# A last stage of attention and recurrence: VectorE takes the gated output earlier in even tiles, and one sum out of PSUM ahead of two statistics

## What is computed

```python
x = x + ln(window_attention(ln(x)))
x = x + ln(mixture_of_experts(ln(x)))        # 2 of 8 experts, and a shared expert
x = x + ln(linear_attention(ln(x)))          # gated, causal
x = x + ln(recurrence(ln(x)))                # two steps of a gated cell, then h
```

```python
y  = w0 * expert0 + w1 * expert1 + shared            # the experts' sums, per token
q, k = rotate(silu(x @ Wq)), rotate(silu(x @ Wk));  v = x @ Wv
out  = causal(q @ k.T) @ v                           # with a running state over chunks
out  = (out @ Wo) * sigmoid(x @ G1 @ G2)             # gated output, then a layer norm
c = f * c + i * tanh(...)                            # gates f, i, twice
h = tanh(x @ wo.T + c @ uo.T + bo)                   # for both halves of the sequence
```

## Time and profile before

| | before |
|---|---|
| median of 3 runs | 1473.22 us (1470.95 to 1474.95) |
| the profiled execution's own time | 1473.82 us |
| its span in the profile | 1472.0 us |
| granted TensorE clock, mean | 0.986 |
| TensorE busy | 1414.0 us (96%) |
| VectorE busy | 870.7 us (59%) |
| ScalarE busy | 714.7 us (49%) |
| GpSimd busy | 603.4 us (41%) |

### The profile page before, as it was taken

The page is one execution under the profiler, slowest core; times in us unless marked ns, Lnnn a source line. Parts: engine busy times, 40 slices in busy tenths (PEclk is TensorE's granted clock), DMA queues, the critical chain, the costliest instruction groups (busy, mean ns, idle before and its releaser), DMA issues. The chain is left out here.

```text
span 1472.0 us, 36241 instructions
## 1 busy us (share of the span) xinstructions
PE 1414.0 (96%) x13257; PEld 1237.0 (84%) x13257; DVE 870.7 (59%) x1979; ACT 714.7 (49%) x1656; POOL 603.4 (41%) x1133
## 2 busy tenths in 40 slices
PE   7999999899999999999999998998999999999995
PEld 6888888788999999999999997876777778777874
DVE  5888887364334433343333331366888888888763
ACT  4666665222444444544445442344555555555543
POOL 3665565124112212111221111545667776775342
PEclk9999999899999999999999999999999999999998
DMA  6434333343111111111111111621121212121000
GB/s 193 121 109 128 113 106 120 92 144 113 37 44 38 43 44 51 41 41 44 44 40 48 44 44 61 184 69 47 42 62 45 62 54 61 45 62 38 9 9 29
DMA packets 88732, 100.10 MB, mean 68 GB/s; under 512 B 12432, under 2 KB 75664, under 8 KB 88560
## 3 DMA queue, kind: packets, MB, share of 16 engines
q1 hardware_dynamic: 80704, 78.51, 17.0%
q0 software_dynamic: 6480, 17.70, 4.2%
q10 hardware_dynamic: 1376, 1.57, 0.3%
HBM read 63.28 MB, written 34.47 MB: 66 GB/s over the span
## 5 line engine op out<-in xcount | busy, mean ns | idle before, releaser
L1049 DVE TENSOR_TENSOR ex_gT<-ex_gT,wa_xk 128x256 f32<-128x256 f32 x71 | 29.9, 421 | 305.7 <-ACT ex_gT L1012 305.7
L913 POOL COPY slot_idx<-source 128x1 int32<-128x1 int32 x69 | 37.4, 542 | 402.8 <-PE wa_Z L971 402.8
L944 PE MATMUL wa_P<-ex_xT,lane_w 128*128 128x128 f32 x1704 | 201.9, 275 | 0.0
L980 PE MATMUL wa_Y<-w,ex_gT 128*128 x852 | 195.7, 379 | 1.6 <-DVE ex_gT L1051 1.6
L944 PEld LDWEIGHTS wa_P<-ex_xT,lane_w 128*128 128x128 f32 x1704 | 196.1, 192 | 0.2 <-issue 0.2
L980 PEld LDWEIGHTS wa_Y<-w,ex_gT 128*128 128x128 f32 x852 | 156.3, 190 | 20.1 <-issue 1.8
L944 PE MATMUL wa_qv<-ex_xT,lane_w 128*128 128x128 f32 x852 | 118.2, 275 | 0.0
L944 PEld LDWEIGHTS wa_qv<-ex_xT,lane_w 128*128 128x128 f32 x852 | 111.9, 192 | 3.6
L940 ACT COPY lane_w<-w 128x1408 f32 x71 | 96.9, 1365 | 7.8 <-issue 1.6
L1010 ACT ACTIVATE ex_gT<-wa_qv 128x256 f32<-128x256 f32 x71 | 27.2, 383 | 130.2 <-PE wa_qv L944 130.1
L1117 POOL TENSOR_SCALAR la_ln_ve<-la_ln_mv 128x1 f32<-128x1 f32 x128 | 33.0, 258 | 139.1 <-DVE la_ln_mv L1110 135.0
(11 more groups left out here) (284 smaller groups left out, 3322.8 us busy)
## 6 DMA issues: line engine op xcount, KB each, us to landing
yg<-ex_yo SPq DMA_DIRECT2D x71, 128.0 KB, 1.7
w<-in_w SPq DMA_DIRECT2D x16, 384.0 KB, 4.9
w<-in_w SPq DMA_DIRECT2D x16, 352.0 KB, 3.1
w<-in_w SPq DMA_DIRECT2D x16, 320.0 KB, 4.0
wa_xa<-in_x SPq DMA_DIRECT2D x32, 128.0 KB, 2.1
x<-wa_xo SPq DMA_DIRECT2D x32, 128.0 KB, 1.7
xn<-wa_xn SPq DMA_DIRECT2D x32, 128.0 KB, 3.7
xn1T<-wa_x1T SPq DMA_DIRECT2D x32, 128.0 KB, 2.1
```

The costliest lines, as they stand in the source:

```text
L913: e.tensor_copy(d["idx"][:], source[:, i:i + 1]).then_inc(S["idx"], 1)
L944: o = e.matmul(out, lane_w[:, i % 2, k, at:at + P], B[i % 2]["xT"][:, k, :], start=(k == 0), stop=(k == KC - 1))
L980: o = e.matmul(yb[:, 0:C], gT[:, k, :], w2[:, bass.ds(KF * y + k, 1), :], start=(k == 0), stop=(k == KF - 1))
```

## The change

Two things move in VectorE's code, and no instruction is added or taken away.

- The gated output `y` (now in a helper, `gated_output`) is issued between the two experts' sums in even tiles. In odd tiles it is issued after the second sum, ahead of that sum's statistics. Before, it stood behind those statistics, and in steps 5 to 8 behind the product `fg` too.
- `ucb` is issued ahead of the statistics with the tags x and 3. Before, it stood behind them. `h` stays behind them.

```diff
+        def gated_output(e, i):
+
+            d = B[i % 2]
+            e.wait_ge(S["z"], i + 1)
+            e.wait_ge(S["gt"], i + 1)
+            e.tensor_tensor(d["y"][:], bE[:, 3, 0:C], d["gt"][:], ALU.mult).then_inc(S["y"], 1)
+
...
+                for i in tile(s, 5, NT):
+                    if i % 2 == 0:
+                        gated_output(e, i)
+                for i in tile(s, 1, NT):
+                    d, t = B[i % 2], i // 2 + i % 2 * PAIRS
                     e.wait_ge(S[f"a1{i % 4}"], 16 * (i // 4 + 1))
                     e.wait_ge(S["y0"], i + 1)
                     e.scalar_tensor_tensor(d["ym"][:], YG[1][i % 4][:], weight[:, 1, t:t + 1], d["ym"][:], ALU.mult,
                                            ALU.add).then_inc(S["y1"], 1)
+                for i in tile(s, 5, NT):
+                    if i % 2:
+                        gated_output(e, i)
+                for i in tile(s, 1, NT):
                     e.wait_ge(S["y1"], i + 1)
-                    norm_stats(e, S, "0", i, d["ln0"], d["ym"][:], 3)
+                    norm_stats(e, S, "0", i, B[i % 2]["ln0"], B[i % 2]["ym"][:], 3)
...
                 for i in tile(s, 5, NT):
-                    d = B[i % 2]
-                    e.wait_ge(S["z"], i + 1)
-                    e.wait_ge(S["gt"], i + 1)
-                    e.tensor_tensor(d["y"][:], bE[:, 3, 0:C], d["gt"][:], ALU.mult).then_inc(S["y"], 1)
                     e.wait_ge(S["y"], i + 1)
-                    norm_stats(e, S, "1", i, d["ln1"], d["y"][:], 2)
+                    norm_stats(e, S, "1", i, B[i % 2]["ln1"], B[i % 2]["y"][:], 2)
...
+                for u in pair(s, 11):
+                    e.wait_ge(S["uo"], u + 1)
+                    e.tensor_tensor(H[u % 2]["ucb"][:], carry_bank(u), bo[:], ALU.add).then_inc(S["ucb"], 1)
                 for i in tile(s, 2, NT):
...
                 for u in pair(s, 11):
                     p = H[u % 2]
-                    e.wait_ge(S["uo"], u + 1)
-                    e.tensor_tensor(p["ucb"][:], carry_bank(u), bo[:], ALU.add).then_inc(S["ucb"], 1)
                     e.wait_ge(S["ucb"], u + 1)
```

## The result

| | before | change |
|---|---|---|
| median, same chip, 16 runs each | 1474.64 us | 1477.38 us |
| lowest to highest | 1470.54 to 1477.99 | 1472.40 to 1482.56 |
| span of the profiled execution | 1472.0 us | 1474.8 us |
| mean granted TensorE clock in it | 0.986 | 0.988 |

The ratio is 1.0026, with a 95% interval of 1.0017 to 1.0035: slower by 2.7 us over the medians. That is less than the 0.3% which the prediction took for what can be told from no change, and yet the interval leaves 1 out. The change's profiled execution took 1476.71 us.

The account below looks back on a forecast made before the run. TensorE, nearly always busy, bounds the kernel, waiting in steady state only for `y`, with VectorE having little room before `em`. Collision 2.7, steps 13 and 31 -0.8, early steps 3.5: +5.4 on 1473.2, so 1478.6 us; range 1472.0 to 1482.5.

Parts of the forecast that it names:

- `y` early, even tiles, "nothing gained": Steady even-tile steps: TensorE's 0.63 us cost of waiting for `y` becomes an equally long wait for `em0`.
- The collision: Steady even-tile steps: GpSimd's final sum holds VectorE's second experts' sum by 0.34 us, +2.7 us over eight steps.
- Steps 13 and 31: Their waits hold 1.1 us more than two common ones; early `y` passes that excess, -0.8 us for both together.
- Early steps: Steps 6, 7, 9 and 11, where TensorE does not wait for `y`: work put ahead of `em` costs +3.5 us.
- Odd-tile steps: Steady odd-tile steps: VectorE some 0.4 us late but within 0.49 of room, so nothing; bound 0.1 in each of ten.
- `ucb`: Early `ucb` is worth nothing by itself; at its old place it would be due just as the candidate gate wants it.
- Rival 1: Even-tile steps: second sum not held, runs in 0.48 us; +2.7 us in all, 1475.9 us; chance 0.28.
- rival 3: TensorE's wait for `y` goes and none takes its place: -7.4 us, 1465.8 us; chance 0.12.
- rival 2: Even-tile second sum held longer: rule's full 0.53, +6.9 us; both halves of GpSimd's sum first, +10.7; chance 0.14.

Follow-up runs that it names:

- the first four experiments: Change plus GpSimd's final sum first, 0.9998; before plus even-tile `y` only, 1.0062; before plus odd-tile `y` and `ucb`, 1.0008; change with old `y` in steps 5 to 12, 1.0017.
- all three edits: The change with GpSimd's final sum ahead of its gathers, `y` early only from step 13, `h` late; 1488.67 us against 1488.13, ratio 0.9992; later chip 0.9982.

## Why the prediction was right, point by point

The forecast was 1478.6 us, 5.4 above the 1473.2 then known; measured was 1477.38, 2.7 above its own comparison. The trace has +5.6 for the steps that the sum speaks of. The mechanism held part by part. That the total came so near has luck in it: two misses in the even-tile steps cancel, and 2.8 us given back in the drain, of which the sum knew nothing, meet a comparison that came out 1.4 us higher than the 1473.2.

- ***`y` early, even tiles, "nothing gained"***: the wait for `y` became one for `em0`. Of the same length to 0.14 us: with no hold the step takes 14.79, not 14.93. Start of `y` after L1381: 1.07 foreseen, 1.06 measured. L1319 after the start of `em`: 0.82 and 0.83.
- ***The collision***: right in place, engine and order, too small in size: 0.49 a step and not 0.34. The order is a matter of 0.09 us, by which GpSimd comes first. What was mis-sized is GpSimd's lead: the sum had 0.18 us (1203.62 to 1203.80). The end came as the `la_c` row has it. The first half of L1785 takes 0.74 us from 1207.84 on, and the second sum ends at 1208.90, 0.32 us behind the end of that half (`la_c`: 0.29). By the letter of the Trainium skill's rule (SBUF — State Buffer, Who interferes with whom), that the first to lock the port keeps it for its whole instruction, the full 0.48 us would have come behind that end. So the trace agrees with the rule in that the one that comes first is not held (the run with `h` moved), and not in the full length after. That 0.49 lies nearer to the 0.53 reckoned by the rule is chance. That one with a single SBUF input does not contend, agrees too: before, `y`, one of whose inputs is in PSUM, starts 0.45 us behind GpSimd's final sum and takes 0.42 us. With the gain of 0.14 above, both misses cancel: +0.35 a step against +0.34, 2.8 for eight steps against 2.7.
- ***Steps 13 and 31***: -0.9 against -0.8. The sum of step 13 is held as well (0.98 us), a ninth time that the prediction did not count; in 31 it is not (0.48), since the final sum, with no gathers ahead of it, is long over.
- ***Early steps***: 0.36, 1.48, 0.81 and 0.45 against 0.6, 1.5, 0.8 and 0.6: 3.1 against 3.5. The count by instructions behind `y` less room held; in steps 6 and 11 the room was a little larger than taken.
- ***Odd-tile steps***: 0.05 each, some 0.6 in all, against nothing, within the bound of 0.1 each.
- ***`ucb`***: nothing by itself, and due as the candidate gate wants it, as one experiment shows (6.5 us of waits without the move).
- **The rivals.** Rival 1 (not held) is out by the 0.97 us of the sum, rival 3 (the wait goes) by the 15.28 us of the step. Rival 1's condition, VectorE first, did occur in the run with `h` moved, by 0.11 us, with the 0.49 us that it had. Of rival 2, the form with the rule's full 0.53 comes near in size, yet its +6.9 is not reached since the rest of the step gained 0.14.
- **The median** is half of what the steps show. In the profiles the difference is clock in the drain, 1.5 us of it in every profile of before and in no other; the prediction has no term for it. On the chips where before takes 1488 us the change costs +0.49% (7 us), because steps of odd tiles and early ones lose more there. The sum was made from rows of the first chip and does not hold for those.

## What to carry to other kernels

An instruction that is pulled ahead of fillers, to end a wait for it, turns the filler's cover into idle time and puts the filler behind itself: sum up what then stands between it and the next instruction that someone waits for, and the room there, before counting the old wait as won. Where VectorE and GpSimd both read two tensors from SBUF, a shift of one against the other by 0.2 us was enough here to create or remove a hold of half a microsecond. So put such a pair where VectorE would be idle anyway, and look for the next collision when a step gets shorter.

## What the runs showed of the hardware

**The hold.** A 0.48 us sum that starts 0.09 us behind a GpSimd sum of two SBUF tensors takes 0.97 us; started 0.11 us ahead of it, it takes 0.49, and the half of GpSimd's sum that starts beside it takes 0.96 instead of 0.74. Instructions of 0.68 and 0.41 us took 1.21 and 0.95 beside two GpSimd sums, and these 1.14 and 1.18 instead of 0.72.

**Pauses of TensorE that nothing in the profile explains.** On the chips where before takes 1487 to 1489 us (three, with profiles of before on two) its odd-tile steps 12 to 28 take 15.3 to 15.5 us, mostly 15.46, where the first chip has 14.52. On the last chip, which has no profile of before, its time is that of the first. In a further profile of before, on such a chip (timeline, TensorE):

```profile
1224.07 0.85 PE L1352 MATMUL la_E<-la_v,la_kr 128*32 128x16 f32 x31
1225.42 0.18 PE L1352 MATMUL la_E<-la_v,la_kr 128*32 128x16 f32 x1 [0.50 <-issue]
1225.53 0.71 PE L1266 MATMUL la_G<-la_wT,gw_wf 128*128 128x128 f32 x4
```

From the start of L1352 to that of L1266 it is 1.46 us, where the first profile has 0.52, and this is the whole difference of the step. TensorE waits for no semaphore there ("issue"). The early steps are longer too, by 5.6 us in steps 5 to 11 of before; in step 7, for one, TensorE takes 1.44 us from L1352 to the next product and not 0.44.

In the change on the same chip the stretch from L1352 to the output product L1381 is longer still: 3.8 us on average in the odd-tile steps 14 to 28, before 3.3, on the first chip 2.4 in both. That makes its odd-tile steps 15.7 to 16.1 us and the change dearer there. The idle time that is booked does not measure it: 5.5 us in 12 at L1352 against 3.6 in 7 before (1056 to 1395 us) on this chip, but 4.9 in 11 against 4.6 in 9 on the next. TensorE's code is the same in the change and in the first four experiments, and yet their odd-tile steps 12 to 28 take anything between 15.2 and 16.1 us.

The place has many short products behind one another, 64 in 1.4 us, and a 16 KB packet of the instruction queue is under way in the pause above (1224.30 to 1225.54). That would fit a late supply of instructions. The other pauses speak against so simple a reading: in the nine odd-tile steps 12 to 28 of this profile they are of one length (1.33 to 1.52 us from L1352 to L1266), and in step 18 no such packet is on the queue from 2.8 us ahead of L1352 to 3.7 us behind it. They stop with the gathers of the experts' rows, whose last ones are in step 29: in steps 30 and 32 of before the stretch takes 0.53 us on every chip. The gathers alone don't make them either, since the first chip has the same gathers and no pause. No run tested any of this, and why chips differ in it stays open.

**Clock after a pause.** After the same 1.8 us of waiting in the drain the granted clock fell to its lower level in all three profiles of before and in none of the eleven of other kernels. After the same 3.4 us it fell in some executions of the same code and not in others. With one code the drain from step 34 on took 82.8 and 84.4 us (the change), and 82.8 and 85.4 (all three edits).
